# Adding the two expert outputs of the last four token groups on TensorE instead of VectorE

## What is computed

```python
topk_w, topk_idx = jax.lax.top_k(probs, TOP_K)          # TOP_K = 2
topk_w = topk_w / jnp.sum(topk_w, axis=-1, keepdims=True)
...
y = jnp.einsum('tei,ehi->teh', jax.nn.silu(h1) * h3, w2)
out = jnp.einsum('te,teh->th', expert_w, y)
...
g = _silu(_L1_ffn_ref(xn, ...))
x = x + s * g
```

## Time and profile before

| | before |
|---|---|
| median of 3 runs | 715.54 us |
| lowest, highest | 714.86, 719.58 us |
| profiled execution | 717.29 us |
| its span | 715.5 us |
| TensorE matmul busy | 598.6 us (84%) |
| VectorE busy | 565.0 us (79%) |
| ScalarE busy | 498.3 us (70%) |
| GpSimd busy | 331.5 us (46%) |
| mean granted TensorE clock | 0.946 |

### The profile page before, as it was taken

How to read it: one execution, slowest core, us unless ns; L and a number is a source line. 1 busy time by engine, 2 the same in 40 slices (tenths; PEclk the granted TensorE clock), 3 DMA queues, 4 the chain that set the end, 5 groups by cost and what they waited for, 6 DMA issues and landing times. The chain is left out here.

```text
span 715.5 us, 16020 instructions
## 1 busy us (share of the span) xinstructions
PE 598.6 (84%) x4825; PEld 357.2 (50%) x4826; DVE 565.0 (79%) x1481; ACT 498.3 (70%) x843; POOL 331.5 (46%) x490
## 2 busy tenths in 40 slices
PE   3578666999999999999999999769994898988960
PEld 2455554233333333333333333748773788887950
DVE  3999997678879797888979776798986576756687
ACT  2367794799989998998989999234452666656631
POOL 0224446234445443434445343425777277755561
PEclk9899986899999999999999999999998899999975
DMA  8000001000666444466665420311222133322465
GB/s 209 15 16 30 30 1 59 1 1 3 112 111 108 97 86 91 65 108 111 111 111 99 94 32 1 146 61 60 85 84 76 38 90 87 91 69 76 130 180 156
DMA packets 76267, 56.06 MB, mean 78 GB/s; under 512 B 6529, under 2 KB 70849, under 8 KB 75969
## 3 DMA queue, kind: packets, MB, share of 16 engines
q1 hardware_dynamic: 70688, 46.01, 29.8%
q0 software_dynamic: 4352, 8.99, 3.7%
q10 hardware_dynamic: 1184, 0.56, 0.3%
HBM read 15.36 MB, written 28.65 MB: 62 GB/s over the span
## 5 line engine op out<-in xcount | busy, mean ns | idle before, releaser
L787 ACT ACTIVATE attend_prob<-attend_ring 128x1024 f32<-128x1024 f32 (+1 forms) x320 | 280.0, 951 | 17.3 <-PE attend_ring L933 15.3
L731 POOL TENSOR_SCALAR_AFFINE_SELECT attend_prob<-attend_prob 128x256 f32<-128x256 f32 x256 | 118.0, 485 | 142.6 <-ACT attend_prob L787 141.8
L953 PE MATMUL attend_ps_o<-attend_prob,attend_v_slot 128*32 128x512 f32 (+3 forms) x1536 | 157.4, 498 | 0.0
L1912 POOL DMA_INDIRECT expert_outputs<-routed_linear_gated,routed_expert_goal_now x72 | 70.1, 973 | 48.3 <-issue 21.5
L933 PE MATMUL attend_ring<-attend_qk_slot 32*128 32x512 f16 (+3 forms) x672 | 80.1, 329 | 8.1 <-ACT attend_prob L787 6.3
L1033 POOL DMA_INDIRECT slots<-rows,slot_index x64 | 62.1, 971 | 35.8 <-issue 33.2
L933 PEld LDWEIGHTS attend_ring<-attend_qk_slot 32*128 32x128 f16 x672 | 22.4, 91 | 106.7 <-ACT attend_prob L787 37.6
L953 PEld LDWEIGHTS attend_ps_o<-attend_prob,attend_v_slot 128*32 128x32 f32 x1536 | 33.7, 108 | 45.2 <-issue 38.0
L1944 DVE SCALAR_TENSOR_TENSOR outed_linear_head_normed<-outed_linear_head_normed,routed_linear_ps_c 128x256 f32<-128x256 f32 x72 | 30.1, 419 | 32.9 <-ACT outed_linear_head_normed L2039 31.8
L2086 PE MATMUL routed_linear_ps_c<-outed_linear_head_normed,head_turned 128*128 128x128 f32 x384 | 52.0, 280 | 0.0
L369 POOL TENSOR_TENSOR project_parts_q<-project_rotated_q,project_parts_q 128x1024 f16<-128x1024 f32 x8 | 17.6, 2202 | 70.5 <-ACT project_parts_q L417 70.5
(11 more groups left out here) (293 smaller groups left out, 1314.0 us busy)
## 6 DMA issues: line engine op xcount, KB each, us to landing
slots<-attend_zeros SPq DMA_DIRECT2D x24, 715.0 KB, 10.0
attend_qk_slot<-qk_parts SPq DMA_DIRECT2D x14, 512.0 KB, 3.1
x_pairs<-slots SPq DMA_DIRECT2D x72, 65.0 KB
v_all<-expert_outputs SPq DMA_DIRECT2D x8, 512.0 KB, 5.6
xn_all<-project_xn SPq DMA_DIRECT2D x8, 256.0 KB, 2.3
w<-w_laid SPq DMA_DIRECT2D x1, 2048.0 KB, 8.0
rows<-rows SPq DMA_DIRECT2D x4, 512.0 KB, 3.7
out<-xn_all SPq DMA_DIRECT2D x8, 256.0 KB, 3.1
```

Of the source, the lines that this page charges most:

```text
L731: ins = nc.gpsimd.affine_select(out=edge, in_=edge, compare_op=ALU.is_ge, fill=0.0, base=0, pattern=[[0, 2], [1, P]], channel_multiplier=-1)
L787: nc.scalar.activation(probs(k, pair)[:, :, 0:width], scores[:, :, 0:width], ACT.Exp, scale=HD ** -0.5).then_inc(exp_made[u][pair], 1)
L953: ins = nc.tensor.matmul(ps_o[RB * s:RB * (s + 1), off:QC], v4[slot][:, j, s], probs(k, s // 2)[:, s % 2, at:at + cols], start=j == 0, sto ...
L1912: pool.indirect_dma_start(m.outputs, bass.IndirectOffsetOnAxis(goal_now[i][:, j:j + 1], 0), y_out[i][:, j * P:(j + 1) * P], None).then_inc ...
```

## The change

For groups 4 to 7 VectorE's `sum_choices` is gone. In its place TensorE, after its last `down`, multiplies each of the two choices by the identity matrix and accumulates both in one bank of PSUM (`add_choices`). Groups 4, 5, 6 and 7 use the four banks that `up` and `turn_x` used before. ScalarE's tanh and VectorE's first `finish` instruction read these banks instead of `y_sum`. ScalarE's `gate` waits also for `gated` of the group that had the `ty` buffer before.

```diff
+    ps_s = [*ps_h, ps_x[0]]
...
+    both = lambda k: ps_s[k % LINE] if k in ends else y_sum[k % LINE]
...
         def finish(k):
 
             dve.wait_ge(ty_made[k % LINE], k // LINE + 1)
-            nc.vector.scalar_tensor_tensor(out=y_sum[k % LINE], in0=ty[k % LINE], scalar=1.0, in1=y_sum[k % LINE], op0=ALU.add,
+            nc.vector.scalar_tensor_tensor(out=y_sum[k % LINE], in0=ty[k % LINE], scalar=1.0, in1=both(k), op0=ALU.add,
...
             for k in ends[::2]:
-                sum_choices(k), sum_choices(k + 1)
                 finish(k), finish(k + 1)
...
         def gate(k):
             act.wait_ge(summed[k % LINE], k // LINE + 1)
-            nc.scalar.activation(ty[k % LINE], y_sum[k % LINE], ACT.Tanh, scale=0.125).then_inc(ty_made[k % LINE], 1)
+            once(act, gated[k % LINE], k // LINE)
+            nc.scalar.activation(ty[k % LINE], both(k), ACT.Tanh, scale=0.125).then_inc(ty_made[k % LINE], 1)
...
+        def add_choices(k):
+
+            pe.wait_ge(y_loaded[k % LINE], 16 * (k // LINE + 1))
+            for w in range(2):
+                ins = nc.tensor.matmul(by_tile(ps_s[k % LINE]), m.ident, choice(k, w), start=w == 0, stop=w == 1)
+            ins.then_inc(summed[k % LINE], 1)
...
         def rest(b):
             expert = experts(pe, b)
             for s in (SB - 2, SB - 1):
                 down(b, s, expert(s + 2))
+            for k in ends:
+                add_choices(k)
```

## The result

The changed kernel took 718.67 us (median of 22 runs, 716.11 to 721.04) against 716.8 us of the kernel before on the same chip (22 runs, 714.86 to 719.58). The ratio is 1.0025, with a 95% interval of 1.0013 to 1.0037: slower by 0.25%, or 1.8 us (0.9 to 2.7). The span of the profiled execution is 717.9 us against 715.5.

What follows compares the result with a forecast made beforehand. Bound taken as last scatter, then loads of groups 6 and 7, then VectorE alone. Slower exposed sums +2.2 us, earlier scatter -0.1, sum +2.1, giving a median of 717.6 us, range 715.4 to 719.3.

Steps and rivals of the forecast that it cites:

- The account of the clock: TensorE at the end: low clock when group 6 lands at 704.77, rising 3.3 to 5.3 us later.
- the prediction's own signs of being wrong: Clock 1.00 at 704.8, sums of 6 and 7 under 4.5 or over 7.5 us, or finish(7) not waiting for TensorE or finish(6).
- The path behind the landing: After group 7's load: 4.83 us on VectorE before the change; with it finish(7) ends 2.0 to 2.7 us later.
- The price of an add: One group's sum on TensorE: 3.64 us at 1.2 GHz, 1.88 at 2.4 GHz, against 0.68 on VectorE.
- The clock at group 6's landing: TensorE at 704.77: taken as low after 1.4 to 2.8 us idle, so group 6's sum takes 3.64 us.
- the likeliest case: End of the kernel: clock low at group 6's start, rising on the way, +1.5 to +2.8 us; chance 0.62.
- The high case: TensorE already at the high clock at 704.77: +0.1 to +0.2 us, or faster by 0.1 to 0.2; chance 0.12.
- The gain of 0.1 us from an earlier last scatter: GpSimd's last scatter without VectorE's sums beside it: landing and both loads up to 0.14 us earlier, taken as 0.1.
- finish and tanh from PSUM: Reading the sums from PSUM: tanh 0.60 us, first finish instruction 0.69 us, no dearer than from SBUF.
- The adds of groups 4 and 5: TensorE from 696.1, done between about 702 and 703.4; the removed 2.76 us of VectorE sums gives nothing.
- The later load: Group 7's load lands up to 1.0 us later through stores; with a high clock +0.9 us, 716.4; chance 0.06.
- The size of the total: Whole kernel: +2.1 us, span from 715.5 to 717.6 us, median 717.6 us.

Runs made afterwards that it cites:

- e7: The changed kernel run again unedited, on another chip than the first comparison: 767.58 us, ratio 1.0020 to the kernel before.
- e3: The changed kernel with 12 unused matmuls of 128 columns on TensorE between the adds of groups 5 and 6: 769.2 us, ratio 1.0022 to the kernel before.
- e2: The changed kernel with only groups 6 and 7 added on TensorE, 4 and 5 back on VectorE: 771.4 us, ratio 1.0039 to the kernel before.
- e1: The changed kernel with only groups 4 and 5 added on TensorE, 6 and 7 back on VectorE: 768.32 us, ratio 0.9992 to the kernel before.
- e5: Second run of e1, groups 4 and 5 on TensorE and 6 and 7 on VectorE: 765.86 us, ratio 0.9971 to the kernel before.
- e8: The changed kernel with group 6 back on VectorE and 20 unused matmuls on TensorE before group 7: 767.71 us, ratio 1.0034 to the kernel before.
- e12: Second run of e3, the changed kernel with 12 unused matmuls between groups 5 and 6: 767.34 us, ratio 1.0034 to the kernel before.
- e11: The changed kernel a third time, unedited, on another chip than the first comparison: 767.14 us, ratio 1.0004 to the kernel before.
- e4: The kernel before, VectorE's four sums kept, plus TensorE's eight matmuls whose results nobody reads: 767.48 us, ratio 1.0003 to the kernel before.
- e6: e1 with groups 6 and 7 multiplied by the attention output before the tanh wait, and VectorE's order changed: 766.22 us, ratio 0.9937 to the kernel before.
- e10: Second run of e6, the reordered version with the multiplication ahead of the tanh wait: 765.82 us, ratio 0.9993 to the kernel before.

## Why the prediction came out as it did

The forecast was 717.6 us with 715.4 to 719.3, no change by 1%, and slightly slower. The changed kernel took 718.67 us, which is 1.1 us over the forecast. The forecast started from 715.54 us, the median of three runs; 22 runs of before gave 716.8, and against these the difference is +1.9 us where +2.1 was forecast. The size and the direction came out. The account of the clock behind them held in one of three profiles of the changed kernel. In the other two, the first profile among them, two of the prediction's own signs of being wrong came true: the clock was 1.00 when group 6 landed, and the sums of 6 and 7 together took 3.70 us, under 4.5. The steps one by one:

- **The path behind the landing** held. The two loads are issued right behind the last landing as before, VectorE now waits for TensorE and ScalarE (3.15 us before finish(6); "about 2" was written, its own times give 2.9), and the part behind VectorE's end is 4.17 us in both profiles.
- **The price of an add** held. Expected were 3.64 us at 1.2 GHz and 1.88 us at 2.4 GHz; measured were 3.78 us (e7) and 1.98 us (e3), and 3.70 us for two groups in a row at the high clock. The Trainium skill's four passes (FP8 and Floating Point Precision, "TensorE Precision Notes") give 1.71 us at 2.4 GHz; the measured 1.98 lies 0.27 above that estimate and 0.10 above the one from the rows.
- **The clock at group 6's landing** is where the likeliest case was only partly right. It was called low. Of three profiles of the changed kernel it was low in one (tail +2.9 us) and high in two (+0.35 and +0.26 us). The high case had a chance of 0.12, which was too small. The step behind it was also off in size: TensorE's idle time was given as 1.4 to 2.8 us and measured 3.54, 3.19 and 3.12 us, because the first two groups took 5.4 to 5.9 us and not up to 7.3. Part of this was a slip: with the clock rising at 699.4, as the prediction allowed, its own prices end group 5 at about 701.5, not 702, and the idle time could be 3.3 us. With so long an idle time the forecast "low" looked safer still, and yet it held in one of three. Where it was low, it also stayed so for longer than forecast: it rose 5.7 us after the first add (e7), where 3.3 to 5.3 had been taken, and the tail grew by 2.9 us, not 2.2; in e2 it rose after 3.5 us.
- **The gain of 0.1 us from an earlier last scatter** failed: the last scatter still takes GpSimd 1.10 us with VectorE's sums gone, as in the earlier trace rows.
- **finish and tanh from PSUM** held: 0.69 and 0.60 us.
- **The adds of groups 4 and 5** held: covered and worth nothing (e1, e5).
- **The later load**, given 0.06, did occur in e3 and e8 by 1.0 and 0.6 us, with its cost exposed as soon as TensorE was fast enough to wait for it. Whether the stores caused it, as the prediction argued, isn't shown. In the changed kernel's own three profiles the load took 5.3 to 5.5 us.
- **The size of the total.** The agreement of the span (717.9 against 717.6) is luck. The profiled execution lost 0.35 us in the tail and had 2.0 us more ahead of it. The mean of the three tails is +1.2 us ((0.35 + 2.9 + 0.26) / 3), the measured total +1.8 (0.9 to 2.7). e2, e3, e12, e7 and e11 show that the tail's cost is real and that the clock sets most of it. Three tails, two of them from other chips, are few for a mean, and 1.2 lies within the interval of the total. Whether the last 0.6 us are chance, the low-clock case being more frequent than one in three, or a small cost upstream, stays open: e1, e4 and e5 see no upstream cost, with intervals of 0.4% to each side. The 2.0 us ahead of the tail in one profile lie within the 4.7 us by which runs of the kernel before differ.

The Trainium skill's advice against idle gaps between matmul bursts (TensorE: Matmul & The Clock Gate, "Why this matters for your kernels") was right in direction, but the prediction leaned on it too far: the page speaks of long gaps only, and the 1.4 to 2.8 us that were forecast did not call for a low clock by it. The traces agree in part: idle times of 3.09 and 3.19 us lowered the clock (e4, e7), idle times of 3.54 and 3.12 us did not. In e4 and e7 the clock was down 2.1 to 2.2 us after the idle time began. The length of the gap alone doesn't tell, and what else decides isn't shown here.

## What to carry to other kernels

Where an operation lies on the path, moving it to an idle engine helps only if that engine's time on the path is shorter than what it replaces: here 0.61 us on VectorE became 2 to 3.8 us on a float32 TensorE that had nothing to do before, and one wait between engines more. On the last microseconds of a program ask first what can be done before the last data lands; taking one multiplication ahead of the wait for the tanh, with the order changed so that VectorE no longer waits for group 7, shortened the tail by 0.8 to 1.1 us (e6 and e10 against e1 and e5), though no total shows it. And where a path runs through a rarely used TensorE, forecast two times, one for each clock, and weigh them. A single time can come out right with the account behind it wrong, as in the first profile here.

## What the runs showed of the hardware

One program gave two tails: eight identical records took 3.70 us or 6.53 us, by the granted clock at their start, and idle times of practically the same length (3.12 and 3.19 us) led to the one and to the other. A load of 512 KB that was issued 0.4 us behind another landed after 6.5 us in e3 and after 5.3 us in e12, which is the same program. The sum of group 5, with two operands in SBUF, took 2.16 us instead of 0.69 beside GpSimd's addition before the change:

```profile
699.04 2.16 DVE L1971 TENSOR_TENSOR routed_linear_qk<-v_all 128x512 f32<-128x512 f32 x1
```

The instruction at 702.16 in the changed kernel, with one operand in PSUM, ran beside the last 0.5 us of GpSimd's addition (701.37 to 702.66) in 0.69 us; that the operand makes the difference isn't tested. And the kernel before took 717 us on one chip and 766 to 768 us on others. Of the changed kernel both chips have a profile: the tails with the high clock agree (11.01 and 10.92 us), and the difference lies in the middle, where L1541 runs from 474.2 to 544.9 us on the one and from 471.8 to 573.6 us on the other (e11), and in the expert stage behind it.
